# Mixture of experts on the chosen pairs only: rows scattered into 23 static tiles of 128, all split weights held in SBUF, results added to the output by accumulating DMAs

## The reference

```
x = x + cross_attention(layernorm(x), context)     # 16 heads, 1601 context rows per batch
x = x + self_attention(layernorm(x))               # causal, 16 heads, 4 key/value heads
h = layernorm(x)
scores = h @ w_gate_router.T                       # 8 experts
topk_scores, topk_idx = top_k(scores, 2); p = softmax(topk_scores)
weights = sum(p[..., None] * one_hot(topk_idx, 8), -2)      # zero for six of eight experts
hidden = silu(h @ w_gate[e].T) * (h @ w_up[e].T)   # per expert e: 512 -> 192, all eight
x = x + sum_e weights[e] * (hidden[e] @ w_down[e].T)        # 192 -> 512
```

## Time and profile before

| quantity | value |
|---|---|
| median of three runs | 1621.39 us |
| profiled execution, whole time | 1622.73 us |
| profiled execution, span of the profile | 1620.9 us |
| TensorE busy | 1539.4 us (95%) |
| VectorE busy | 847.4 us (52%) |
| ScalarE busy | 740.6 us (46%) |
| GpSimd busy | 464.6 us (29%) |
| moved by DMA | 53.81 MB, mean 33 GB/s |
| cross-attention, last matmul about | 1199 us |
| self-attention, last matmul ends about | 1379 us |
| expert matmuls | 1404 to 1618 us |

### The profile page before, as it was taken

How to read it: one execution, slowest core, us unless ns; L and a number is a source line. 1 busy time by engine, 2 the same in 40 slices (tenths; PEclk the granted TensorE clock), 3 DMA queues, 4 the chain that set the end, 5 groups by cost and what they waited for, 6 DMA issues and landing times. The chain is left out here.

```text
span 1620.9 us, 41874 instructions
## 1 busy us (share of the span) xinstructions
PE 1539.4 (95%) x16226; PEld 1301.7 (80%) x16226; DVE 847.4 (52%) x1793; ACT 740.6 (46%) x1515; POOL 464.6 (29%) x492
## 2 busy tenths in 40 slices
PE   5789999999999999999999999999987998899999
PEld 2378888888888888888888888888865666899998
DVE  6755555555655555555564555555525554433333
ACT  2245555555555555555555555555532322311111
POOL 3233333333333333333333333333331000022102
PEclk9989999999999999999999999999988999699999
DMA  6021011000110100011000110100020000111011
GB/s 232 17 93 32 15 29 32 17 26 27 32 28 15 32 27 28 16 30 28 27 19 27 28 32 15 28 27 16 3 60 1 0 0 1 60 59 59 20 39 52
DMA packets 35920, 53.81 MB, mean 33 GB/s; under 512 B 7091, under 2 KB 15670, under 8 KB 35766
## 3 DMA queue, kind: packets, MB, share of 16 engines
q1 hardware_dynamic: 35332, 51.44, 10.4%
q10 hardware_dynamic: 434, 0.08, 0.0%
HBM read 48.89 MB, written 2.62 MB: 32 GB/s over the span
## 5 line engine op out<-in xcount | busy, mean ns | idle before, releaser
L1042 POOL TENSOR_TENSOR ksq<-kc 128x512 f32<-128x512 f32 x200 | 208.4, 1042 | 445.3 <-DVE kc L1087 443.4
L1087 DVE TENSOR_TENSOR kc<-psum,bk_sb 128x512 f32<-128x512 f32 x200 | 138.2, 691 | 235.1 <-PE psum L100 235.1
L954 ACT COPY v_sb<-psum 128x512 f32<-128x512 f32 x192 | 112.6, 587 | 292.8 <-PE psum L100 292.8
L968 ACT ACTIVATE probs<-psum 128x1024 f32<-128x1024 f32 x208 | 202.9, 1023 | 89.3 <-PE psum L1209 88.9
L1209 PE MATMUL psum<-qbd,k 64*128 64x128 f32 x3328 | 217.4, 280 | 4.2 <-issue 4.1
L1209 PEld LDWEIGHTS psum<-qbd,k 64*128 64x128 f32 x3328 | 196.2, 188 | 11.2 <-issue 6.9
L1035 POOL TENSOR_TENSOR y_lo<-y_sb,y_hi 128x256 fp32r<-128x256 f32 x190 | 139.6, 735 | 226.6 <-ACT y_hi L927 225.7
L1226 PEld LDWEIGHTS psum<-v_sb,probs 128*64 128x64 f32 x6144 | 187.3, 138 | 17.6 <-issue 17.5
L1226 PE MATMUL psum<-v_sb,probs 128*64 128x33 f32 x6144 | 198.0, 224 | 0.0
L1093 DVE TENSOR_REDUCE kss<-ksq 128x16 f32<-128x512 f32 x200 | 136.5, 682 | 111.4 <-POOL ksq L1042 111.4
L100 PE MATMUL psum<-wk_hi,y_hi 128*128 128x512 f32 x400 | 176.8, 442 | 10.8 <-issue 8.7
(11 more groups left out here) (223 smaller groups left out, 2310.9 us busy)
## 6 DMA issues: line engine op xcount, KB each, us to landing
y_sb<-in_y SPq DMA_DIRECT2D x48, 512.0 KB, 3.8
expert_raw<-in_wg SPq DMA_DIRECT2D x5, 768.0 KB, 4.6
expert_raw<-in_wu SPq DMA_DIRECT2D x5, 768.0 KB, 4.6
expert_raw<-in_wd SPq DMA_DIRECT2D x5, 768.0 KB, 4.5
out_dram<-x_sb SPq DMA_DIRECT2D x8, 256.0 KB, 2.0
x_sb<-in_x SPq DMA_DIRECT2D x1, 1536.0 KB, 10.4
wq<-in_wq SPq DMA_DIRECT2D x4, 256.0 KB, 4.7
xa_wo<-in_wo SPq DMA_DIRECT2D x1, 1024.0 KB, 12.2
```

Of the source, the lines that this page charges most:

```text
L968: nc.scalar.activation(probs[:, buf(u), :], psum[:, bank:bank + 2, :].rearrange("p a n -> p (a n)"), ACT.Exp, scale=SCALE).then_inc(s["ex" ...
L1042: nc.gpsimd.tensor_tensor(sq[:, buf(n)], kc[:, buf(n)], kc[:, buf(n)], ALU.mult).then_inc(s["ksq"], 1)
L1087: nc.vector.tensor_tensor(kc[:, buf(n)], psum[:, K_BANK, :], g.bk[:], ALU.add).then_inc(s["kb"], 1)
```

## The change

Routing moves from the expert stage into self-attention. Round i's two tiles are routed in round i+1, the last two after the last round, and the hardware loop of `rounds` is replaced by four rounds written out. For its two tiles a round has: `route_norm` (statistics, reciprocal root, normalised rows), two `route_turn` (4 transposes each), two `router` (4 matmuls each of 8 columns), `route_top` (the two largest scores and their experts), `ranks` (4 matmuls with a triangle of ones and with ones: how many earlier tokens chose each expert), `route_place` (each pair's row number), `route_rows` (token number, both weights and first expert behind the row), and on GpSimd four indirect DMAs that scatter 128 rows of 516 floats into `slots` in DRAM. There each expert owns a region of 1024 rows. After the last round `route_tables` makes, with some 26 small VectorE operations each waiting for the one before, four tables for 23 tiles: the first row, the weight block, the column of the down weights' rest and the count of experts that must be split.

`slots` has to be blank before: during cross-attention SP writes it with rows of zeros and a token number past the output, 2.1 MB in one DMA for each pair of batches and 1.8 MB once, together 18.7 MB.

The tokens' residual `g.x` is stored to the output by SP in self-attention, behind `residual2`. The expert stage then has 23 tiles (2048 pairs need 16 full ones, and each of 8 experts may leave one partly filled, so 23 always suffice, and all 23 are always computed). For a tile SP reads its first row from the table and loads 128 rows. TensorE reads three values from the tables (`steer`), transposes the rows (`turn`), and issues 12 matmuls of 384 columns (gate and up side by side) and, a tile late, 6 of 512 columns, with register addresses for the weights, and 2 transposes of the hidden rows. ScalarE scales the result by the row's weight (`scale`), and GpSimd adds the 128 rows to the output in DRAM by an indirect accumulating DMA, which waits for the one before to have landed (`add`). The output array gets 128 rows more, where blank rows are added. The weights of all eight experts stay split in SBUF. They are loaded expert by expert (1 MB), two in self-attention, the others in the expert stage, where ScalarE makes the high parts and VectorE the low parts (2048 columns each), six of them between the tiles, after tiles 0, 1, 2, 4, 5 and 6 (`AFTER`). The diff, cut:

```diff
+GATE_UP = KD * 2 * F
+WHALF = GATE_UP + D
+WBLOCK = 2 * WHALF
+REGION = T
+TILES = 2 * T // P + E_ - 1
+SLOT_ROWS = E_ * REGION + (E_ - 1) * P
+ROW = D + 4
+PICK = 2
+CONSTS = P + NT + 2 * E_ + 2 * TILES
...
+                def blanks(first, n):
+                    sp.dma_start(io["slots"][bass.ds(first, n * P), :].rearrange("(n p) c -> p n c", p=P),
+                                 blank[:].unsqueeze(1).to_broadcast([P, n, ROW])).then_inc(s["blank"], 16)
+                blanks(E_ * REGION, E_ - 1)
...
                     context(i, 1)
+                    blanks(i * REGION, REGION // P)
...
+                sp.dma_start(consts[:], io["route"]).then_inc(s["r_consts"], 16)
+                sp.dma_start(wr[:], io["wr"].rearrange("(k p) n -> p k n", p=P)).then_inc(s["r_wr"], 16)
+                for e in range(2):
+                    load_expert(sp, io, g.raw[:, e, :], e).then_inc(s["raw"], 16)
+                for i in range(NT // 2):
+                    for u in range(2):
+                        t = i * 2 + u
+                        sp.wait_ge(s["x2"], done(i, u))
+                        sp.dma_start(io["out"][t * P:(t + 1) * P, :], g.x[:, t, :]).then_inc(s["out"], 16)
...
+                for i in range(R):
+                    pool.wait_ge(s["r_place"], i + 1)
+                    pool.wait_ge(s["r_rows"], i + 1)
+                    for u in range(2):
+                        for n in range(PICK):
+                            nc.gpsimd.indirect_dma_start(
+                                io["slots"][:, :], bass.IndirectOffsetOnAxis(ap=target[:, i, n, u:u + 1], axis=0),
+                                rows[:, u, :], None).then_inc(s["r_slots"], 16)
...
+                def route_norm(i):
...
+                    if i:
+                        dve.wait_ge(s["r_slots"], 16 * i * 2 * PICK)
+                    for u in range(2):
+                        nc.vector.tensor_scalar(rows[:, u, 0:D], g.x[:, i * 2 + u, :], rmv[:, i, u, 0:1], rrs[:, i, u:u + 1],
+                                                ALU.subtract, ALU.mult).then_inc(s["r_xn"], 1)
...
+                def route_top(i):
+                    dve.wait_ge(s["r_logits"], i + 1)
+                    for u in range(2):
+                        last = nc.vector.max(out=top[:, i, u, :], in_=logits[:, i, u, :])
+                    link(last)
+                    for u in range(2):
+                        last = nc.vector.max_index(out=idx[:, i, u, :], in_max=top[:, i, u, :], in_values=logits[:, i, u, :])
+                    nc.vector.tensor_tensor(gap[:, i], top[:, i, :, 1], top[:, i, :, 0], ALU.subtract).then_inc(s["r_gap"], 1)
+                    link(last)
+                    link(nc.vector.tensor_copy(chosen[:, i], idx[:, i, :, 0:PICK]))
+                    for n in range(PICK):
+                        last = nc.vector.tensor_tensor(pick[:, i, n], ids.unsqueeze(1).to_broadcast([P, 2, E_]),
+                                                       spread(chosen[:, i, :, n], E_), ALU.is_equal)
+                    link(last)
+                    nc.vector.tensor_tensor(both[:, i], pick[:, i, 0], pick[:, i, 1], ALU.add).then_inc(s["r_both"], 1)
...
+                    dve.wait_ge(s["r_pf"], i + 1)
+                    bank = psum[:, ROUTE, RANKS:RANKS + 3 * E_]
+                    nc.vector.tensor_tensor(count[:, i + 1], count[:, i], bank[:, 2 * E_:3 * E_], ALU.add).then_inc(s["r_count"], 1)
+                    link(nc.vector.tensor_tensor(rank[:, i], bank[:, 0:2 * E_].rearrange("p (u e) -> p u e", u=2),
+                                                 count[:, i].unsqueeze(1).to_broadcast([P, 2, E_]), ALU.add))
+                    for n in range(PICK):
+                        last = nc.vector.tensor_tensor(found[:, i, n], pick[:, i, n], rank[:, i], ALU.mult)
+                    link(last)
+                    link(nc.vector.tensor_reduce(place[:, i].rearrange("p n u -> p (n u)"),
+                                                 found[:, i].rearrange("p n u e -> p (n u) e"), AX_X, ALU.add))
+                    nc.vector.tensor_copy(target[:, i], place[:, i]).then_inc(s["r_place"], 1)
...
+                def route_tables():
...
+                    bank = psum[:, ROUTE, RANKS:RANKS + 3 * E_]
+                    pe.matmul(bank[:, 0:2 * E_], before_me, both[:, i].rearrange("p u e -> p (u e)"), start=True, stop=False,
+                              skip_group_check=True)
+                    pe.matmul(bank[:, E_:2 * E_], ones[:], both[:, i, 0], start=False, stop=True, skip_group_check=True)
+                    pe.matmul(bank[:, 2 * E_:3 * E_], ones[:], both[:, i, 0], start=False, stop=False, skip_group_check=True)
+                    pe.matmul(bank[:, 2 * E_:3 * E_], ones[:], both[:, i, 1], start=False, stop=True, skip_group_check=True)\
+                        .then_inc(s["r_pf"], 1)
...
+        ORDER = (0, 1, 0, 1, 2, 0, 1, 2)
+        TURN = (0, 0, 1, 1, 1, 2, 2, 2)
+        AFTER = (0, 0, 0, 1, 2, 4, 5, 6)
+        def table(eng, name, j, low, top):
+            return eng.value_load(t[name][0:1, j:j + 1], min_val=low, max_val=top)
...
+                def rows_in(j):
+                    first = table(sp, "first", j, 0, SLOT_ROWS - P)
+                    if j >= XB:
+                        sp.wait_ge(s["add"], 16 * (j - XB + 1))
+                    sp.dma_start(rows[:, j % XB, :], io["slots"][bass.ds(first, P), :]).then_inc(s[f"rows{j % XB}"], 16)
...
+                def add(j):
+                    pool.wait_ge(s["y"], j + 1)
+                    if j:
+                        pool.wait_ge(s["add"], 16 * j)
+                    nc.gpsimd.indirect_dma_start(
+                        io["out"][:, :], bass.IndirectOffsetOnAxis(ap=rows[:, j % XB, D:D + 1].bitcast(U32), axis=0),
+                        y[:, j % 2, :], None, compute_op=ALU.add).then_inc(s["add"], 16)
...
+                def scale(j):
+                    act.wait_ge(s["dn"], j + 1)
+                    act.wait_ge(s["weight"], j + 1)
+                    if j >= 2:
+                        act.wait_ge(s["add"], 16 * (j - 1))
+                    nc.scalar.activation(y[:, j % 2], psum[:, DN + j % 2, :], ACT.Identity, scale=weight[:, j % 2]).then_inc(s["y"], 1)
...
+                for j in range(TILES + 1):
+                    if 0 < j and j + 1 < TILES:
+                        x_high(j + 1)
+                    if j < TILES:
+                        silu(j)
+                    if j:
+                        scale(j - 1)
+                    if j < TILES:
+                        h_high(j)
+                    for e in range(2, E_):
+                        if AFTER[e] == j:
+                            high(e)
...
+                def hidden(j):
+                    dve.wait_ge(s["gate"], j + 1)
+                    if j >= 2:
+                        dve.wait_ge(s["th"], j - 1)
+                    up = psum[:, GU + j % 2, F:2 * F]
+                    nc.vector.tensor_tensor(hid[:, j % 2, 0:P], gate[:, j % 2, 0:P], up[:, 0:P], ALU.mult)
+                    for n, name in enumerate(("lower", "upper")):
                         last = nc.vector.scalar_tensor_tensor(
...
+                            out=hid[:, j % 2, P + n * 64:P + (n + 1) * 64], in0=gate[:, j % 2, P:F],
+                            scalar=t[name][:, j:j + 1], in1=up[:, P:F], op0=ALU.mult, op1=ALU.mult)
+                    last.then_inc(s["hid"], 1)
...
+                def gate_up(j, base, need):
+                    pe.wait_ge(s["xhi"], j + 1)
+                    pe.wait_ge(s["xlo"], j + 1)
+                    pe.wait_ge(s["wlo"], need)
+                    if j >= 2:
+                        pe.wait_ge(s["hid"], j - 1)
+                    terms = [(x_hi[:, j % 2, k, :], x_lo[:, j % 2, k, :], w[:, bass.ds(base + k * 2 * F, 2 * F)],
+                              w[:, bass.ds(base + (WHALF + k * 2 * F), 2 * F)]) for k in range(KD)]
+                    split_product(pe, psum[:, GU + j % 2, 0:2 * F], terms).then_inc(s["gu"], 1)
...
+                def steer(j):
+                    return (table(pe, "block", j, 0, (E_ - 1) * WBLOCK), table(pe, "at", j, 0, (E_ // 2 - 1) * D),
+                            table(pe, "need", j, 1, E_))
+                held = [steer(0)]
+                turn(0)
+                for j in range(TILES + 1):
+                    if j + 1 < TILES:
+                        held.append(steer(j + 1))
+                        turn(j + 1)
+                    if j < TILES:
+                        gate_up(j, held[j][0], held[j][2])
+                    if j:
+                        down(j - 1, held[j - 1][0], held[j - 1][1])
+                    if j < TILES:
+                        turn_hidden(j)
...
+        "experts": np.concatenate([gate_up, wd[:, 0:P]], 2),
+        "wd_rest": np.concatenate([wd[:E_ // 2, P:F], wd[E_ // 2:, P:F]], 1).swapaxes(0, 1),
```

(41 more changed lines are left out.)

542 lines of the change are left out of this document (293 added, 249 removed).

## The result

The changed kernel takes 1742.22 us (median of 4 runs, 1740.33 to 1743.87) against 1621.29 us for the kernel before (4 runs): ratio 1.0743, 95% interval 1.0730 to 1.0757. It is 7.4% slower. The forecast was 1580, faster, with a range to 1645: wrong in direction and outside the range.

A forecast was written before the change was run, and what follows sets the result against it. TensorE was taken to bound the 241 us from the last `residual2` on; these become 191, with 9 added ahead. 1388.5 + 24.3 + 14.3 + 141.9 + 2 + 8.6 = 1579.6 in the span, so 1580 us, range 1535 to 1645.

The forecast's parts named there:

- step 6: Accumulating DMA on GpSimd: 23 adds form a chain, each 5.4 us, less than the tile period, so covered.
- step 5: Tile period in the expert stage: 4.13 us TensorE, 0.2 uncovered, 2.1 register reads; 6.45 us with rounding.
- L: Length of one accumulating DMA with its making and hand-over, not in the trace: taken as 5.4 us.
- Rival C: Chain of accumulating DMAs sets the period, deciding from 6.45 us an add, slower from 8.2; chance 0.16.
- Rival B: TensorE's clock falls in the tiles: 1669 us at 1.2 GHz throughout, 1625 for half the time; chance 0.13.
- Rival A: TensorE's register reads are cheap, so the DMA chain's 5.4 us is the period: 1557 us; chance 0.25.
- Step 1: Three routings inside self-attention: 3.0 us more a round on TensorE, VectorE's work hidden; +9.0 us, bounds +5 and +20.
- 2, blanking: Blanking `slots` during cross-attention, 18.7 MB more on mostly idle DMA engines: cost 0, bounds 0 and +8 us.
- step 3: Last routing, bare after the last `residual2`: 24.3 us, bounds 20 to 33, replacing the 24.8 of before.
- Step 4: Start of the expert stage, splitting first weights until tile 0's hidden rows are turned: 14.3 us, bounds 10 and 20.
- 5 to 7, the tiles: Expert stage: 22 periods of 6.45 us (141.9), adds covered, plus 2 us for splitting six experts between tiles.
- Step 8: End of the kernel, last down matmuls, scale and accumulating DMA after the last tile: 8.6 us.

The follow-up runs named there:

- static: Changed kernel with five row buffers and constant weight addresses in place of TensorE's register reads (fixed experts): 1555.92 us (one run).
- b_unroll: Kernel before, with the self-attention rounds written out and no routing in them: 1622.27 us, ratio 1.0003.
- ring5: Changed kernel with five row buffers in place of three, nothing else: 1569.81 us, ratio 0.9684 to the kernel before.
- one_read: Changed kernel with five row buffers and one TensorE register read a tile in place of three: 1561.43 us, ratio 0.9617 to the kernel before.
- one_read6: Changed kernel with six row buffers and one TensorE register read a tile: 1562.73 us, ratio 0.9630 to the kernel before.
- two_reads_b: Changed kernel with six row buffers and two TensorE register reads a tile in place of three: 1564.29 us (one run).

## Why the prediction was wrong

**The step that failed is step 6, and through it the period of step 5.** Step 6 named `scale(j)`, `y`, `down(j)` and `rows_in` as what follows an add, and then compared only the add's own length with the period: "5.4, less than the period, so it's covered." That test is right for a chain of adds alone. What follows the add leads back to the next add, through the row load, the turn and 18 matmuls of another tile, and the length to compare was that of the whole loop, divided by the tiles that share it. The prediction's own durations, with 0.3 for hand-overs, would have given it: 5.4 (L) + 2.0 (load) + 0.43 (turn) + 3.48 (12 and 6 matmuls) + 0.6 (scale) + 0.3 (hand-overs) = 12.2 us, shared by one tile with three buffers and the turn ahead of `down`. 22 x 12.2 in place of 141.9 makes the time about 1707, slower by 5%. The rest of the measured 14.8 is mostly the load (2.7 for 2.0) and, at a clock of 0.69, the turn and the matmuls (1.1 and 5.0 to 5.8 for 0.43 and 3.48).

**Rival C** stood on the right side with the wrong price. It put the point of decision at an add of 6.45 us and the loss at 8.2; the add measured 4.8 and the loss came all the same. Its sign, "`scale` and SP's row loads wait for the add", is what the trace shows for SP, but TensorE's gap was before `turn` and not before `down`. No rival had the loop in it, so the prediction had no price for a kernel 7% slower; its 0.23 for slower rested on other causes.

**Rival B**, the clock, is a follower here: 0.69 where TensorE is busy for 44% of the window, in single gaps of 8.4 us; with five buffers (1416 to 1562) it is 0.94. By the durations above it adds 2 to 3 us to a loop of 14.8, an estimate, and doesn't make it. **Rival A** is what `static` shows: without reads the period is the DMA chain, 5.5 us (forecast 5.4), the time 1556 (forecast 1557). That the times agree so well is in part luck, since in `static` tile 0's hidden rows were turned 9 us earlier than forecast, while the end took longer.

**The other terms**, of the forecast's span of 1579.6 and the measured 1741.4:

| step | forecast | measured | difference |
|---|---|---|---|
| 1, three rounds longer | +9.0 | +9.0, less 7.2 at the start of the stage | -7.2 |
| 2, blanking | 0 | +0.3 at the end of cross-attention | in the row above |
| 3, last routing | 24.3 | 23.3 | -1.0 |
| 4, start of the expert stage | 14.3 | 13.8 | -0.5 |
| 5 to 7, the tiles | 143.9 | 309.0 | +165.1 |
| 8, the end | 8.6 | 14.0 | +5.4 |

The sum of the differences is 161.8. Step 1's rounds came out right in their sum (rounds 0 to 3 are 0.2, 2.9, 4.0 and 1.9 us longer than the same rounds of the kernel before; the written-out form costs nothing, as `b_unroll` shows); which operation makes them longer wasn't tried. What it overlooked is what a moved piece of work takes along: the splits that left GpSimd had been slowing VectorE. Step 4's reason was only half right: the last thing awaited there was the load of the down weights' rest (5.82 us) and its two splits. Step 5's own terms are good: TensorE 4.12 us (forecast 4.13), nothing uncovered (0.2), three reads 1.6 (2.1), so a steady 5.9 with five buffers where 6.45 was forecast. Step 6's L was 4.8 to the landing; with the hand-over, which the forecast of 5.4 had in it, 5.5 on GpSimd and 5.0 on SP. Step 8 is longer because the last two adds queue behind each other, 5.5 us apart. With two more buffers the forecast of 1580 would have been 0.6% from the 1569.81 measured. Some of that is luck: in `ring5` the tiles began 7 us earlier than forecast and took 10 us less (134 for 143.9), and the end took 4.5 us more. Still, the single durations were mostly good, and what failed was the graph between them.

Two small slips of the working changed nothing: step 3's terms add up to 24.2 and not 24.3, and with half of (B)'s 0.13 and part of (C) faster, the share of the others in "faster" should have been over 0.06 and not 0.02.

## What to carry to other kernels

Where a buffer stays in use until a late step has finished (here: row numbers read by the last DMA of a tile), write down the loop buffer free → load → compute → last use, add up its length, and divide by the number of tiles that share it. That number is the ring's size less the tiles by which the order of an in-order engine puts new work ahead of old. Compare this quotient with the engines' period before any single transfer. It costs a line to widen a ring (three to five: 172 us) or to move an early step behind a late one (124 us). When work moves off an engine, look at what stood beside it there.

## What the runs showed of the hardware

- An indirect DMA of 128 rows of 2 KB to DRAM lands 2.7 us after its issue, the accumulating one 4.8, and GpSimd spends 0.96 and 1.56 us of that on making them. One after the other the accumulating ones come every 5.5 us, since GpSimd issues the next some 0.7 us behind the landing; SP's row load that waits for the same landing is issued 0.14 us behind it.
- The making of such a DMA can be held up by VectorE. With one read and five buffers, the timeline of VectorE and GpSimd:

```profile
1448.02 2.29 DVE L2120 TENSOR_TENSOR experts<-expert_raw,experts 128x2048 fp32r<-128x2048 f32 x1 [1.38 <-ACT experts L2034]
1448.29 3.44 POOL L2020 DMA_INDIRECT out_dram<-x_sb,moe_rows  x1 [5.43 <-DMA out_dram<-x_sb,moe_rows]
...
1453.96 2.29 DVE L2120 TENSOR_TENSOR experts<-expert_raw,experts 128x2048 fp32r<-128x2048 f32 x1 [1.38 <-ACT experts L2034]
1455.78 1.91 POOL L2020 DMA_INDIRECT out_dram<-x_sb,moe_rows  x1 [4.04 <-DMA out_dram<-x_sb,moe_rows]
```

  The making takes 3.44 and 1.91 us instead of 1.56, and in both cases it ends 1.4 us after VectorE's subtraction of two SBUF inputs does (1450.31 and 1451.73; 1456.25 and 1457.69). So it is in all nine cases in which a making began beside such a subtraction, three each in `one_read`, `one_read6` and `two_reads_b`. In `static` three makings had begun 0.3, 0.8 and 1.2 us ahead of one (at 1443.60, 1449.10 and 1454.61), and took 1.55 and 1.56 as ever. Up to 1.9 us of the chain of adds is lost at such a place. No run moved the subtractions away. The Trainium skill (SBUF — State Buffer, Who interferes with whom) says of a `tensor_tensor` that it takes only the read interface of the shared pair, and infers that the making of descriptors needs the write interface, so that the one doesn't hold up the other. For an indirect DMA these nine cases speak against that.
- Reading table values into TensorE's registers, just ahead of the matmuls that need them, left TensorE idle for 1.6 us with three reads, 0.93 with two and 0.28 with one: 0.6 to 0.7 us for each further read. Where TensorE stands still for something else just before, the one read can't be seen.
- The granted clock stood lower where TensorE's gaps were long. In the changed kernel's tiles, with gaps of 8.1 to 8.6 us between stretches of 6 to 7, its mean was 0.69, a mixture of the levels 1.2 and 2.4 GHz; in `one_read`, with gaps of at most 1.6 us, it was full from 1450 to 1550:

```profile
1450.00:1550.00 100.00, 76.92 (x417) 65.18 (x415) 39.76 (x128) 35.86 (x73) 28.99 (x18) 1.00 0.53 88
```
